# A two-layer perceiver block on one core: the small stages of each half of the batch cut into numbered fine slots, TensorE one pair behind, and half 1's first part moved among half 0's second part

## The chip, the core and the metric

The kernel runs on one core of a Trainium2 chip. Its time is in microseconds of the device (us); lower is better. Before the change three timed runs gave 323.14, 327.37 and 328.0 us, with a median of 327.37 us. Everything is float32.

## What is computed

The input is a batch of 16 sequences of 32 tokens with 128 features, a context of 512 keys for each sequence, and a mask over the keys. Six blocks follow each other, each with a layer norm ahead and a residual behind it:

```python
x = x + L0_xattn(layernorm(x), ctx)        # 16 heads of 8; query i sees its own 16 keys only
x = x + L0_attn(layernorm(x))              # time mixing, projections k, v, r, a scan over 32 steps
x = x + L0_ffn(layernorm(x))               # 8 experts of 64 (top 2 by sqrt(softplus)) and a shared one
x = x + L1_xattn(layernorm(x), ctx, mask)  # full attention, 16 heads, 512 keys
x = x + L1_attn(layernorm(x))              # linear attention with relu features, then a gelu layer of 512
x = x + L1_ffn(layernorm(x))               # 16 experts of 512, top 1, capacity 32 tokens
```

The scan keeps a running maximum o and two sums p and q, and gives `(A p + B v) / (A q + B)`, multiplied by a sigmoid of r.

## The kernel before

The program is written engine by engine, with semaphores by hand; each engine works strictly through its own list. The batch is cut into two halves of 8 sequences (256 tokens, two tiles of 128). Stretches of heavy work alternate on TensorE, and the small stages of a half (chains of little steps that go from engine to engine) are woven into them:

- `local(h)` is the first attention of half h: for each sequence a product on VectorE (L746), the softmax, a widened probability (L312), and the context product on TensorE (L1184). Between them stand the projections of the context to keys and values (`projection`, L1147 and L1151), 32 in all; the last 9 of them come after `local(1)`.
- `small_stages(h)` holds the rest of layer 0 and the queries of layer 1. Its first part is the residual and norm, the mixes (L809), the scans (L814, L830, L834) and the quotient with its reciprocal (L844). Its second part is the projection back, norm, the router (L860 to L890), the experts' hidden layer (Silu, L581), their second layer (L1302 to L1305), norm and the query (L1314, L912, L913).
- `full` is the attention of layer 1 over 64 units (4 heads of one sequence each), two to a pair, 32 pairs. For a pair: scores on TensorE (L1334), mask and minimum on VectorE (L941), the exponential on ScalarE (L601), four transposes per unit on TensorE (L1344), a copy by ScalarE (L608) or VectorE (L950), and three pairs later the product with the values (L1359). `take_heads` (L922, L924) empties the bank of outputs every eight pairs.
- `linear_stages(h)` is the rest of layer 1 from the inverse sums of the softmax (L966, L1383) through linear attention, the gelu layer (L1442, Gelu at L637, L1451, Gelu at L641) and the gate (L1040 to L1053) to the slots of the dispatch.
- A tail of 16 experts ends the program (L1535 to L1562).

The small stages are Python generators on each engine: each `yield` ends a coarse step, and the surrounding loop decides when the next one is written into the list. There is a step for each unit of `full` on every engine at the same place of the loop, so that TensorE, ScalarE, VectorE and GpSimd reach a step at about the same time and wait inside it for each other:

```python
if u < UNITS:
    advance(second, 1)
if u == UNITS - 1:
    finish(second)
if u >= LINEAR:
    advance(first, 1 if u % 5 != 4 else 0)
```

Here `second` is half 1's small stages, in units 0 to 31, and `first` half 0's linear stages, from unit 40. Half 0's small stages go into `local(1)`, and what is left of them stands behind it alone; half 1's stand whole in `full`; half 0's linear stages stand in the second part of `full` up to the gate, and what is left goes into `last_stages` with half 1's. `keep_warm` writes matmuls without use (L1498) where TensorE is otherwise alone with a chain. The banks X, Y and Z take the small products of both halves in turn.

## Time and profile before

| | us |
|---|---|
| median of three runs | 327.37 |
| the profiled execution's own time | 319.62 |
| its span, first to last instruction | 317.6 |
| TensorE busy | 281.4 (89%) |
| VectorE busy | 189.4 (60%) |
| ScalarE busy | 139.3 (44%) |
| GpSimd busy | 27.9 (9%) |
| mean granted clock of TensorE | 0.936 of full speed |

PE is TensorE, DVE VectorE, ACT ScalarE, POOL GpSimd. PEclk is the clock granted to TensorE as a share of 2.4 GHz; it has two levels, 2.4 and 1.2 GHz, so a stretch with a mean of c ran (1 - c) times 2 of its length at the lower one. A float32 matmul shows as several passes, so counts in the trace are twice those of the program. A bracket at a row's end is the idle time of the engine just before it, and what ended it.

### The profile page before, as it was taken

The page shows a single profiled execution, that of the slowest core. Times are in us where ns is not written, and L with a number is a line of the kernel's source. Part 1 is how long each engine was busy: PE and PEld are TensorE (multiplying, and loading weights), DVE is VectorE, ACT ScalarE, POOL GpSimd, SP SyncE. Part 2 cuts the span into 40 slices and gives each one's busy share as a digit, 9 for nine tenths or more (in the row PEclk, how much of TensorE's full clock was granted, in tenths as well). Part 3 has the DMA queues.
Part 4 walks back from the last instruction along what each step waited for, and adds up shares of the span by engine and source line. Part 5 has one row for each costly group of instructions (what it writes and reads, how often), then busy time and mean ns, then how long its engine had stood idle before and what let it go on. Part 6 is the DMA issues. An engine that isn't in the chain of part 4 may idle for free.

```text
span 317.6 us, 5216 instructions
## 1 busy us (share of the span) xinstructions
PE 281.4 (89%) x1990; PEld 181.5 (57%) x1990; DVE 189.4 (60%) x507; ACT 139.3 (44%) x296; POOL 27.9 (9%) x47
## 2 busy tenths in 40 slices
PE   8998999687988866997989999988899959979996
PEld 6325876166877543554566555454556528667766
DVE  3555265877443487975454668776753774742572
ACT  1215533454650374579713677375368800132130
POOL 4000000000030400013001200000100001010000
PEclk9999999999997999599565999999969989999999
DMA  7999290000019100050005000000000294000001
GB/s 288 427 439 398 66 198 3 0 1 2 0 43 417 70 1 2 0 134 0 0 3 132 3 0 2 2 1 0 2 0 2 91 436 169 1 2 0 0 2 35
DMA packets 3400, 26.79 MB, mean 84 GB/s; under 512 B 432, under 2 KB 1456, under 8 KB 1840
## 3 DMA queue, kind: packets, MB, share of 16 engines
q1 hardware_dynamic: 3376, 26.47, 23.0%
q8 instruction: 16, 0.26, 0.3%
q14 instruction: 8, 0.07, 0.1%
HBM read 26.20 MB, written 0.26 MB: 83 GB/s over the span
## 4 chain that ended last, share of the span: by engine, by line
PE 41%; DVE 9%; issue 5%; ACT 5%; POOL 1%; POOLq 0%; DVEq 0%; ACTq 0%
PE bank L1344 8%; PE bank L1334 8%; PE bank L1359 5%; PE bank L1498 3%; PE bank L1128 1%; PE bank L1305 1%; PE bank L1562 1%; PE bank L1417 1%; PE bank L1383 1%; PE bank L1553 1%; PE bank L1535 1%; PE bank L1442 1%; PE bank L1118 1%; ACT L601 1%; ACT work_sb L601 1%
## 5 line engine op out<-in xcount | busy, mean ns | idle before, releaser
L601 ACT ACTIVATE work_sb<-work_sb,small_sb 128x512 f32<-128x512 f32 x48 | 34.7, 722 | 45.6 <-DVE small_sb L941 45.4
L941 DVE CUSTOM_DVE_ANT_0 work_sb<-bank,mask_sb 128x512 f32<-128x512 f32 x48 | 31.9, 689 | 17.3 <-PE bank L1334 16.8
L1334 PE MATMUL bank<-k_sb,work_sb 32*128 32x512 f32 x128 | 40.2, 706 | 0.6 <-DVE small_sb L941 0.5
L1344 PEld LDWEIGHTS bank<-early_sb,work_sb 128*128 128x128 f32 x192 | 22.4, 151 | 30.3 <-issue 16.6
L1344 PE MATMUL bank<-early_sb,work_sb 128*128 128x128 f32 x192 | 33.9, 305 | 1.1 <-ACT work_sb L608 1.1
L374 POOL TENSOR_TENSOR rstd_sb<-veps_sb,minus_half_sb 128x2 f32<-128x2 f32 (+1 forms) x13 | 10.1, 774 | 214.9 <-DVE veps_sb L701 171.3
L1359 PE MATMUL bank<-work_sb,v_sb 128*32 128x128 f32 x512 | 22.6, 300 | 4.5 <-DVE otmp_sb L922 2.8
L608 ACT COPY work_sb<-bank 128x512 f32<-128x512 f32 x40 | 22.7, 568 | 6.6 <-PE bank L1344 6.6
L1498 PE MATMUL bank<-early_sb 128*128 128x256 f32 x98 | 25.0, 397 | 0.0
L950 DVE COPY work_sb<-bank 128x512 f32<-128x512 f32 x24 | 16.5, 688 | 11.5 <-PE bank L1344 9.8
L1498 PEld LDWEIGHTS bank<-early_sb 128*128 128x128 f32 x98 | 18.9, 203 | 3.1 <-issue 0.8
L746 DVE SCALAR_TENSOR_TENSOR work_sb<-bank,early_sb,work_sb 128x512 f32<-128x512 f32 x16 | 12.0, 749 | 14.4 <-PE bank L1207 13.9
L1359 PEld LDWEIGHTS bank<-work_sb,v_sb 128*32 128x32 f32 x512 | 13.4, 116 | 10.7 <-issue 7.9
L1151 PEld LDWEIGHTS bank<-late_sb,ctx_sb 128*128 128x128 f32 x128 | 16.2, 191 | 3.5 <-issue 3.4
L1147 PE MATMUL bank<-ctx_sb,early_sb 128*128 128x512 f32 x32 | 15.9, 615 | 1.7 <-ACT k_sb L503 1.7
L1151 PE MATMUL bank<-late_sb,ctx_sb 128*128 128x128 f32 x128 | 17.1, 277 | 0.3 <-DVE v_sb L784 0.2
L1207 PE MATMUL bank<-ctx_sb,early_sb 128*128 128x512 f32 x32 | 16.1, 604 | 0.2 <-DVE work_sb L746 0.2
L503 ACT ACTIVATE k_sb<-bank,early_sb 128x512 f32<-128x512 f32 x16 | 10.7, 684 | 9.8 <-PE bank L1147 9.7
L1334 PEld LDWEIGHTS bank<-k_sb,work_sb 32*128 32x128 f32 x128 | 10.6, 202 | 7.0 <-issue 4.6
L523 ACT COPY work_sb<-bank 128x512 f32<-128x512 f32 x16 | 9.4, 586 | 10.7 <-PE bank L1184 10.7
L1344 PE MATMUL bank<-early_sb,spare_sb 128*128 128x128 f32 x64 | 11.4, 307 | 2.6 <-ACT work_sb L608 2.6
L312 DVE TENSOR_TENSOR work_sb<-bank,early_sb 128x512 f32<-128x512 f32 x16 | 10.1, 684 | 5.9 <-PE bank L1171 3.2
(234 smaller groups left out, 454.3 us busy)
## 6 DMA issues: line engine op xcount, KB each, us to landing
ctx_sb<-moe_w SPq DMA_DIRECT2D x1, 4096.0 KB, 12.0
k_sb<-moe_w SPq DMA_DIRECT2D x1, 4096.0 KB, 13.6
ctx_sb<-ctx SPq DMA_DIRECT2D x3, 1024.0 KB, 14.1
late_sb<-late SPq DMA_DIRECT2D x1, 2895.0 KB, 20.6
mask_sb<-ctx_tok SPq DMA_DIRECT2D x1, 2048.0 KB, 12.3
v_sb<-ctx_tok SPq DMA_DIRECT2D x1, 2048.0 KB, 26.9
mask_sb<-mask SPq DMA_DIRECT2D x4, 512.0 KB, 8.1
mask_sb<-mask SPq DMA_DIRECT2D x8, 256.0 KB, 4.6
```

The costliest lines, as they stand in the source:

```text
L601: s.activation(sc[u % NSC], sc[u % NSC], ACT.Exp, bias=smin[:, u:u + 1], scale=-1.0, accum_out=rsum[:, u:u + 1]).then_inc(sig("p1_ready"), 1)
L608: s.copy(pt[j % NPT], bank[2 + j % NT][:, :]).then_inc(sig("pT_act"), 1)
L746: v.scalar_tensor_tensor(prod[c % HB].rearrange("p (q j) -> p q j", j=LOCAL), bank[c % 2][:, :].rearrange("p (q j) -> p q j", j=LOCAL), wt ...
L941: v.tensor_tensor_reduce(sc[u % NSC], bank[SB[u % NS]][:, :], mask[:, KEYS * b:KEYS * (b + 1)], MASK_BIG, 3e38, ALU.add, ALU.min, smin[:, ...
L950: v.tensor_copy(pt[j % NPT], bank[2 + j % NT][:, :]).then_inc(sig("pT_dve"), 1)
L1147: last = mm(dst[:, :], wt("wk1"), ctx[:, KEYS * b:KEYS * (b + 1)], start=True, stop=True)
L1151: last = mm(dst[:, P * k:P * (k + 1)], ctx[:, at:at + P], wt("wv1"), start=True, stop=True)
L1207: mm(bank[c % 2][:, :], wt("wk0"), ctx[:, KEYS * c:KEYS * (c + 1)], start=True, stop=True).then_inc(sig("k0_ps"), 1)
L1334: mm(bank[SB[u % NS]][:, :], qc[b][r, :], k1[r, KEYS * b:KEYS * (b + 1)], start=True, stop=True)\
L1344: last = nc.tensor.transpose(bank[2 + u % NT][:, P * k:P * (k + 1)], sc[u % NSC][:, P * k:P * (k + 1)], wt("ident"))
L1359: last = mm(bank[4][r, at:at + P], vkey[:, b, k, r], pt[(GROUPS * b + g) % NPT][:, P * k:P * (k + 1)], start=(k == 0), stop=(k == KT - 1), ...
L1498: mm(bank[2][:, 0:256], wt("ident"), wt("wv0")[:, 0:256], start=True, stop=True)
```

## The change

Every `yield` of the small and linear stages is replaced by `yield from rest(n)`, so that a stage has a number of fine slots, and the same piece of work has a number that agrees over the engines: 70 slots for the small stages, 63 for the linear ones. Long steps are cut (the norm into three pieces, the reciprocal into two, the scaled hidden tiles into two pairs, and so on). The loops now give three slots to a pair, and TensorE does the slots of pair v in round v + 1:

```diff
-        def beside(u, second, first):
-            if u < UNITS:
+        LOCAL_SLOTS = 3
+        SMALL_MIXED, SMALL_SLOTS = 27, 70
+        LOCAL_DONE = LOCAL_SLOTS * HB + 3 + 2 * (HB - NE + 1)
+        LINEAR_FROM, LINEAR_TO = 2 * HB + LATE_OUT, PAIRS + 1
+        def beside(v, i, second, first):
+            if v <= PAIRS // 2 - 2:
                 advance(second, 1)
-            if u == UNITS - 1:
-                finish(second)
-            if u >= LINEAR:
-                advance(first, 1 if u % 5 != 4 else 0)
+                if v == PAIRS // 2 - 2 and i == 2:
+                    finish(second)
+            if LINEAR_FROM <= v <= LINEAR_TO:
+                advance(first, 1)
+        def both_small(first, second, then):
+            for k in range(SMALL_SLOTS - LOCAL_DONE):
+                advance(first, 1)
+                if k < SMALL_MIXED:
+                    advance(second, 1)
+                then(k)
+            finish(first)
         def last_stages(first, second):
-            for k in range(STAGES):
+            for k in range(LINEAR_SLOTS):
                 advance(second, 1)
-                if k in (4, 8, 11):
+                if k % 5 in (0, 2, 4):
                     advance(first, 1)
+                if k == LINEAR_SLOTS // 2:
+                    finish(first)
             finish(second)
...
-            local(1, stages, pace_local)
-            finish(stages)
+            local(1, small0)
+            both_small(small0, small1, lambda k: projection() if k % 3 == 1 and nproj[0] < len(PROJ) else None)
             first = linear_stages(0)
-            full(small_stages(1), first)
+            full(small1, first)
```

`LOCAL_DONE` is 37: half 0's small stages have done 37 slots when `local(1)` ends. `both_small` then writes the 33 left, each followed (for the first 27) by a slot of half 1, and a context projection in every third. In `full` the remaining 43 slots of half 1 stand at pairs 0 to 14, and the first 45 slots of half 0's linear stages at pairs 19 to 33 (up to the gelu layer's second product); the other 18 slots go into `last_stages`, three in five of half 1's slots.

On TensorE the loop of `full` becomes:

```diff
+                    if 1 <= w <= LINEAR_TO + 1:
+                        beside(w - 1, 0, second, first)
                     if LATE_OUT <= w < PAIRS + LATE_OUT:
                         outputs((w - LATE_OUT) // 2, (w - LATE_OUT) % 2)
-                    if w <= PAIRS:
-                        beside(2 * w, second, first)
-                        if w:
-                            turn(2 * w - 1)
-                        beside(2 * w + 1, second, first)
+                    if 1 <= w <= LINEAR_TO + 1:
+                        beside(w - 1, 1, second, first)
+                    if 1 <= w <= PAIRS:
+                        turn(2 * w - 1)
+                    if 1 <= w <= LINEAR_TO + 1:
+                        beside(w - 1, 2, second, first)
```

To let two halves stand among each other, buffers are doubled: half 1's first part uses banks 0 and 1 in place of X and Y, the hidden tiles and the transposed weights have a place for each half, the linear stages use bank 3 and X or Y by half for their last products, and the residual semaphores are counted by half. On ScalarE the logarithm and all five Silu now stand in one slot:

```diff
                 act.wait_ge(sig("w_ready"), h + 1)
                 s.activation(fr[4], fr[3], ACT.Ln).then_inc(sig("ln_ready"), 1)
-                yield
-                for n in range(5):
-                    act.wait_ge(sig("hid_ps"), 3 * h + (1, 1, 2, 2, 3)[n])
+                silu(0, X[:, 0:HTOK], 2)
+                silu(1, X[:, HTOK:], 2)
+                silu(4, Y[0:H0, HTOK:], 1)
+                silu(2, X[:, 0:HTOK], 3)
+                silu(3, X[:, HTOK:], 3)
```

Three places show what this does to the lists. The first is VectorE between the experts of half 0 and the first scores. Before (L898 scales the hidden tiles, L734 to L715 are residual and norm, L912 and L913 the query, L941 the first unit of `full`):

```order
L893 COPY mask_sb<-bank 8x256
L898 TENSOR_TENSOR mask_sb<-mask_sb,bank 128x256 x4
L734 TENSOR_TENSOR x_tok_sb<-bank,xb_tok_sb 128x256
L694 BN_STATS stats_sb<-x_tok_sb 128x6 x2
L697 BN_AGGR aggr_sb<-stats_sb 128x2 x2
L701 TENSOR_SCALAR veps_sb<-aggr_sb 128x2
L715 TENSOR_SCALAR xn_tok_sb<-x_tok_sb,aggr_sb,rstd_sb 128x128 x2
L912 TENSOR_SCALAR work_sb<-bank,late_sb 128x256
L913 TENSOR_SCALAR work_sb<-work_sb 128x256
L941 ISA work_sb,small_sb<-bank,mask_sb 128x512
```

The same place after, from the second pair of scaled tiles on (mask_sb rows are half 1's scan stage, L745 is a projection's copy):

```order
L867 TENSOR_TENSOR otmp_sb<-otmp_sb,bank 128x256 x2
L790 TENSOR_TENSOR mask_sb<-mask_sb 128x8x32
L795 TENSOR_TENSOR mask_sb<-mask_sb 128x8x32
L796 SCALAR_TENSOR_TENSOR mask_sb<-mask_sb 128x264
L799 TENSOR_TENSOR mask_sb<-mask_sb 128x256
L800 SCALAR_TENSOR_TENSOR mask_sb<-mask_sb 128x264
L745 COPY v_sb<-bank 128x512
L693 TENSOR_TENSOR x_tok_sb<-bank,xb_tok_sb 128x256
L648 BN_STATS stats_sb<-x_tok_sb 128x6 x2
L802 TENSOR_TENSOR mask_sb<-mask_sb 128x256
L803 TENSOR_TENSOR mask_sb<-mask_sb 128x256
L654 BN_AGGR aggr_sb<-stats_sb 128x2 x2
```

Half 1's scans moved in between half 0's scaled tiles and its residual, and its sums in between the pieces of the norm.

The second is ScalarE at half 1's router. Before (L573 is the logarithm, L581 the five Silu, L601 an exponential of `full`):

```order
L571 ACTIVATE small_sb<-small_sb 128x16
L573 ACT_TABLE_LOAD
L573 ACTIVATE small_sb<-small_sb 128x16
L601 ACT_TABLE_LOAD
L601 ACTIVATE work_sb,small_sb<-work_sb,small_sb 128x512
L581 ACT_TABLE_LOAD
L581 ACTIVATE mask_sb<-bank,late_sb 128x256 x4
L581 ACTIVATE mask_sb<-bank,late_sb 64x256
L601 ACT_TABLE_LOAD
L601 ACTIVATE work_sb,small_sb<-work_sb,small_sb 128x512
```

And after (L551 the logarithm, L557 the Silu, L575 the exponential):

```order
L575 ACTIVATE spare_sb,small_sb<-spare_sb,small_sb 128x512
L551 ACT_TABLE_LOAD
L551 ACTIVATE small_sb<-small_sb 128x16
L557 ACT_TABLE_LOAD
L557 ACTIVATE mask_sb<-bank,late_sb 128x256 x2
L557 ACTIVATE mask_sb<-bank,late_sb 64x256
L557 ACTIVATE mask_sb<-bank,late_sb 128x256 x2
L575 ACT_TABLE_LOAD
L575 ACTIVATE work_sb,small_sb<-work_sb,small_sb 128x512
```

The exponential between the logarithm and the Silu is gone, and with it one load of a table; the others stand in one block.

The third is TensorE at the end of `full`. Before (L1359 outputs, L1467 the gate of half 0, L1383 the start of half 1's linear stages):

```order
L1359 MATMUL bank<-work_sb,v_sb 32x128 x8
L1467 MATMUL bank<-late_sb,lnT_sb 128x16 x2
L1344 MATMUL bank<-early_sb,work_sb 128x128 x8
L1359 MATMUL bank<-work_sb,v_sb 32x128 x8
L1344 MATMUL bank<-early_sb,spare_sb 128x128 x4
L1359 MATMUL bank<-work_sb,v_sb 32x128 x16
L1383 MATMUL bank<-mask_sb,late_sb 32x256 x4
```

And after (L1335 outputs, L1426 and L1438 the two products of the gelu layer of half 0, L1362 the start of half 1's linear stages):

```order
L1335 MATMUL bank<-work_sb,v_sb 32x128 x8
L1426 MATMUL bank<-lnT_sb,late_sb 128x256 x4
L1335 MATMUL bank<-work_sb,v_sb 32x128 x8
L1438 MATMUL bank<-late_sb,mask_sb 128x128 x8
L1362 MATMUL bank<-mask_sb,late_sb 32x256 x4
L1478 MATMUL bank<-early_sb 128x256 x2
```

The gelu layer of half 0 moved from the middle of the last pairs to behind the last scores, and half 0's gate is no longer in `full`.

## Rows read from the trace of the kernel before

**Rows 1.** The busy time of each engine by stage of the program.
```profile
core 0: us, PE busy (x) PEld busy (x) DVE busy (x) ACT busy (x) POOL busy (x), PEclk, DMA share, GB/s
...
81.65:108.23 26.58, 23.85 (x137) 19.61 (x136) 10.76 (x35) 10.00 (x17) 5.06 (x5) 0.94 0.39 158
108.23:183.66 75.43, 66.39 (x464) 39.00 (x463) 50.75 (x146) 43.41 (x101) 10.58 (x16) 0.82 0.12 29
183.66:195.05 11.39, 11.29 (x114) 6.07 (x113) 8.76 (x22) 8.34 (x22) 0.00 (x0) 1.00 0.00 0
195.05:256.85 61.80, 54.51 (x479) 32.78 (x478) 40.55 (x117) 36.91 (x84) 3.11 (x4) 0.94 0.09 35
256.85:299.63 42.78, 36.67 (x188) 28.39 (x187) 22.77 (x76) 7.48 (x15) 3.11 (x4) 0.96 0.19 81
```

**Rows 2.** Two stretches of the first pairs, same columns.
```profile
120.00:133.50 13.50, 10.94 (x84) 6.05 (x84) 12.53 (x29) 7.03 (x17) 0.72 (x1) 0.75 0.00 0
147.60:174.35 26.75, 23.46 (x128) 15.13 (x125) 12.29 (x37) 13.07 (x28) 2.80 (x3) 0.62 0.17 39
```

**Rows 3.** TensorE in order of time: start, us, engine, line, tiles, count.
```profile
149.67 0.65 PE L1281 MATMUL bank<-lnT_sb,late_sb 128*64 128x256 f32 x2 [2.05 <-ACT mask_sb L581]
151.08 2.08 PE L1334 MATMUL bank<-k_sb,work_sb 32*128 32x512 f32 x4
...
180.79 1.13 PE L1334 MATMUL bank<-k_sb,work_sb 32*128 32x512 f32 x4
...
230.67 0.65 PE L1359 MATMUL bank<-work_sb,v_sb 128*32 128x128 f32 x16 [1.93 <-DVE otmp_sb L922]
```

**Rows 4.** ScalarE at half 1's logarithm and Silu; four such loads stand there.
```profile
143.82 1.28 ACT L573 ACT_TABLE_LOAD   x1
...
148.78 2.04 ACT L581 ACTIVATE mask_sb<-bank,late_sb 128x256 f32<-128x256 f32 x5
```

**Rows 5.** VectorE during half 1's first part: all, then L941, then L950.
```profile
110.59:134.40 23.81, 20.60 (x56) 0.86 0.00 1
110.59:134.40 23.81, 6.63 (x22) 0.86 0.00 1
110.59:134.40 23.81, 2.15 (x4) 0.86 0.00 1
```

**Rows 6.** VectorE's longest waits in half 0's second part.
```profile
90.34 0.29 DVE L882 TENSOR_TENSOR mask_sb<-small_sb 128x128 f32<-128x128 f32 x1 [3.02 <-POOL small_sb L439]
...
101.75 0.42 DVE L734 TENSOR_TENSOR x_tok_sb<-bank,xb_tok_sb 128x256 f32<-128x256 f32 x1 [5.04 <-PE bank L1305]
```

**Rows 7.** TensorE on half 1's first part: L1128, then L1247, in one stretch.
```profile
109.20:120.00 10.80, 0.71 (x4) 1.00 0.01 2
109.20:120.00 10.80, 1.56 (x6) 1.00 0.01 2
```

**Rows 8.** VectorE at the end of `full`: all, then L941, then L950.
```profile
242.80:257.29 14.49, 9.79 (x35) 1.00 0.38 145
242.80:257.29 14.49, 3.92 (x12) 1.00 0.38 145
242.80:257.29 14.49, 2.07 (x3) 1.00 0.38 145
```

**Rows 9.** TensorE: half 0's gate, the last outputs, and a gelu layer's second product.
```profile
249.37 0.59 PE L1118 MATMUL bank<-early_sb,xn_tok_sb 128*128 128x128 f32 x2 [0.29 <-DVE xn_tok_sb L715]
...
252.11 0.62 PE L1467 MATMUL bank<-late_sb,lnT_sb 128*128 128x16 f32 x4
...
255.77 1.08 PE L1359 MATMUL bank<-work_sb,v_sb 128*32 128x128 f32 x32 [0.88 <-DVE work_sb L950]
259.94 2.07 PE L1383 MATMUL bank<-mask_sb,late_sb 128*32 128x256 f32 x8 [3.09 <-DVE mask_sb L966]
...
286.83 2.05 PE L1451 MATMUL bank<-late_sb,mask_sb 128*128 128x128 f32 x16
```

794 lines of the change are left out of this document (373 added, 421 removed).

## The prediction

> **What bounds the kernel now.** I read the busy time of each engine by stage first [rows 1]; the limits differ between the stages. To 81.65 us the two local attentions run, which the change touches only in where half 0's steps stand. From 81.65 to 108.23 TensorE works on half 0's second part and on projections. From 108.23 to 256.85 `full` runs: 16 pairs with half 1's small stages (75.43 us), 4 pairs with nothing beside them (11.39 us), and 12 pairs with half 0's linear stages and the last outputs (61.80 us). Half 1's linear stages end at 299.63, and the tail of 17.97 us to the end of the span is not touched.
>
> The four bare pairs tell what a pair costs: 11.39 / 4 = 2.85 us, with TensorE busy for 11.29 of 11.39. So `full` is bound by TensorE where nothing stands in its way. I therefore split its 148.62 us into work at full clock, idle time of TensorE, and time lost to the clock. Idle is 75.43 - 66.39 = 9.04, 0.10, and 61.80 - 54.51 = 7.29: 16.4 us. A stretch at half clock takes twice its time, so the loss is (1 - granted clock) times the stretch: 0.18 x 75.43 = 13.6, and 0.06 x 61.80 = 3.7: 17.3 us. What is left, 114.9 us, is work. The 33.7 us of idle and clock are what the change can win in `full`.
>
> Where they come from stands in the order of time. The clock was 0.75 from 120.0 to 133.5 and 0.62 from 147.6 to 174.35 [rows 2]; at 151.08 the four passes of a pair's scores took 2.08 us, at 180.79 1.13 us [rows 3]. The longer stretch began while TensorE waited 2.05 us at L1281 for ScalarE, which stood at its Silu between loads of tables [rows 3, 4]. At 230.67 TensorE had waited 1.93 us for `take_heads`, which stood on VectorE behind a whole norm that waited for GpSimd [rows 3]. These are coarse steps in which one engine waits for the next, and everything queued behind the wait waits too.
>
> **`full`.** What leaves: half 1's first part. On TensorE that is 0.71 (L1128) + 0.59 (one turned norm, priced by the row at 249.37) + 1.56 (three mixes) = 2.9 us [rows 7, 9]. Half 0's gate leaves too, 0.59 + 0.62 = 1.2 us [rows 9]. Work falls to 114.9 - 4.1 = 110.8 us. No matmul is added; three slots a pair instead of two units a pair only spread the same ones.
>
> Idle: TensorE's slots stand a pair later than those of the others, so their results have about one pair, 2.85 us, to arrive. Against that, VectorE now waits for TensorE's answer in the same way, but behind its wait stand only the second unit's minimum and one copy, while the next scores need just the first unit's minimum. Load is no limit: VectorE was busy 50.75 of 75.43 us and loses half 1's first part. One stall I can name stays: ScalarE has the logarithm, five Silu and the return to the exponential in one block. By the rows it takes 3 x 1.28 (loads) + 0.2 (the logarithm over 16 columns, an estimate: under the 0.4 us of one Silu) + 2.04 = 6.1 us [rows 4], and the last two Silu wait for a product that TensorE may only start after the first two. TensorE has about 2.9 us of other work meanwhile, so some 3 to 4 us are lost. For the rest I take half of what there was; idle 10 us in all. Its ends: 5 us (little but that block) and 16.4 us (nothing gained).
>
> Of tables, each load here took 1.28 us and the next instruction followed at once [rows 4]. The Trainium skill (ScalarE: Activation LUTs, What ACT_TABLE_LOAD costs) states about 2.66 us for each switch, a drain included. By it the block would be 3 x 2.66 + 2.3 = 10.2 us, as an estimate from that page, and the stall some 4 us longer; the trace disagrees with it. The same page (Table sets) has logarithm and exponential in one set, so that moving the logarithm would save nothing; here both directions cost a load.
>
> Clock: half of the causes go (the first part with its scans, the norm ahead of `take_heads`, and ScalarE's three further switches for the gelu layer, which now stands behind the last exponential). The ScalarE block may bring the clock down once more. I take 9 us of the 17.3; the ends are 3 and 17.3. So `full` takes 110.8 + 10 + 9 = 129.8 us, 18.8 less than now.
>
> **Half 0's second part, now with half 1's first.** VectorE was busy 10.76 of 26.58 us here [rows 1]. It gets half 1's first part: 20.60 - 6.63 - 2.15 = 11.8 us [rows 5]. The sum, 22.6 us, still fits in 26.6, and its waits are long enough to hold it: 5.04 us for the experts' products and 3.02 us for GpSimd's power are the largest [rows 6]. But the order is fixed, and half 1's steps also stand right ahead of steps on which half 0 depends, for instance the scans ahead of the residual and the sums between the pieces of the norm. If two thirds are covered, a third of 11.8 shows: +4 us. TensorE's 2.9 us go into its own waits, instead of matmuls without use. Ends: 0 (all covered) and 11.8 + 2.9, about +15 (nothing covered). I take 4, since the 15.8 us in which VectorE had nothing are more than what comes.
>
> **Half 1's linear stages.** They get the 18 last slots of half 0's. On VectorE that is 9.79 - 3.92 - 2.07 = 3.8 us [rows 8], beside 22.77 of 42.78 busy [rows 1]: half of it on the chain, 1.9 us. At the start the chain ran from the last outputs at 256.85 to L1383 at 259.94, an idle wait of 3.09 us [rows 9]. Now half 0's second gelu product (2.05 us by the row at 286.83) stands between, behind a load of 1.28 us and four gelu on ScalarE, so L1383 comes about 1.6 us later. Together +3.5 us; ends 0 and 8.
>
> **The local attention.** Half 0's steps are finer and some stand earlier; nothing is added. 0, between -2 and +2.
>
> **The sum.** -18.8 + 4 + 3.5 + 0 = -11.3 us. Against the profiled execution's own 319.62 us (2.0 more than its span) this gives 308.3. That execution was 7.8 us faster than the median of the three runs, 327.37; the difference taken off the median gives 316.1, and I predict 316.
>
> **Rivals.**
> - *The clock stays.* Low clock comes again at the ScalarE block and at the thin products of the router, since no matmul that follows it changed. For it: both times that half 0 or half 1 reached its experts, the stage showed less than full clock (0.94, 0.62 [rows 1, 2]). Against it: the pairs stand thicker around them. Loss stays 17.3: `full` gains 148.6 - (110.8 + 10 + 17.3) = 10.5, the sum is -10.5 + 7.5 = -3.0, so 324.4.
> - *Two chains in one line.* In the mixed stage each in-order engine stands at the one half's wait while the other half's work is ready behind it, so that the chains add up rather than overlap. Half 1's first part took 23.8 us in `full` [rows 5]; all of it on top of 26.6 costs +23.8. Sum: -18.8 + 23.8 + 3.5 = +8.5, so 335.9, slower. It decides from the point where the mixed stage is over 26.6 + 15.3 = 41.9 us long. For it: the fixed order. Against it: 15.8 us without work on VectorE, and slots whose numbers leave two to six slots between a request and its use.
> - *All of it.* Idle 5, clock 3, the mixed stage +2 and the last +1.5: `full` 118.8, sum -29.8 + 3.5 = -26.3, so 301. Against it: the ScalarE block alone makes idle time.
>
> **How the numbers follow.** My forecast has 0.55, with its own range 310 to 323; the clock stays 0.23; two chains in one line 0.10; all of it 0.12. The range from 305 to 329 takes in most of the second and the upper half of the last. A measurement here can tell about 2% from no change, so faster means under 320.8 and slower over 333.9. Faster is most of the forecast (0.48), all of it (0.12) and a little of the clock case (0.03): 0.63. Slower is the line of two chains, 0.10; the rest, 0.27, is within 2%.
>
> **What would show it.** In the profile after: the first scores at 112 us rather than 108; `full` near 130 us, with TensorE idle about 10 us of it and a granted clock around 0.93; the idle row ahead of the second hidden product (L1247 of the new program) 2 us or more; from the end of `full` to the end of the linear stages 46 us. Wrong would be: a mixed stage over 42 us long, a clock under 0.90 in the first 16 pairs, or idle time of TensorE on VectorE's minima (L915) of more than 5 us, which would say that VectorE now waits too long between a pair's two units.

## The result and the profile after

The changed kernel took 332.32 us, the median of four runs (332.00 to 333.74); the kernel before, run beside it, took 326.05 (323.14 to 328.00). The ratio is 1.031, with a 95% interval from 1.025 to 1.037: slower, where faster by three to four per cent was predicted, and outside the range of 305 to 329. Single executions of one kernel can be several per cent longer at a lower granted clock, so each ratio, here and below, sets only the executions without that against such ones of the kernel before, while the medians are over all; where a run had a single one of them, no ratio is given.

The sum of the prediction was made against one profiled execution, and so is this one. I cut both traces at four events on TensorE: the end of the last product with the values of `local(1)`, the first scores, the end of the last outputs, and the last dispatch. The busy time of the changed kernel between them, and in two stretches of its first pairs:

```profile
core 0: us, PE busy (x) PEld busy (x) DVE busy (x) ACT busy (x) POOL busy (x), PEclk, DMA share, GB/s
84.06:135.80 51.74, 37.71 (x165) 29.90 (x163) 22.24 (x64) 12.82 (x25) 7.59 (x7) 0.80 0.16 62
135.80:264.39 128.59, 117.31 (x1019) 67.79 (x1018) 84.16 (x236) 80.22 (x191) 10.36 (x11) 0.93 0.16 50
264.39:312.32 47.93, 43.45 (x224) 34.64 (x224) 26.41 (x95) 10.08 (x20) 3.81 (x5) 0.96 0.12 51
159.89:170.00 10.11, 9.25 (x40) 5.11 (x40) 3.37 (x11) 6.89 (x15) 1.41 (x1) 0.54 0.00 0
177.00:183.50 6.50, 6.50 (x34) 3.04 (x32) 4.39 (x9) 2.59 (x6) 0.00 (x0) 0.55 0.00 0
```

And of the kernel before, from the same event (in the prediction the stage was cut 0.9 us later, [rows 1]):

```profile
80.75:108.23 27.48, 24.75 (x139) 20.03 (x139) 10.76 (x35) 10.48 (x18) 5.06 (x5) 0.94 0.38 153
```

| part | before | after | difference | predicted |
|---|---|---|---|---|
| to the end of the values | 80.75 | 84.06 | +3.3 | 0 (-2 to +2) |
| half 0's second part, in the new program with half 1's first | 27.48 | 51.74 | **+24.3** | +4 (0 to +15) |
| `full` | 148.62 | 128.59 | **-20.0** | -18.8 |
| half 1's linear stages | 42.78 | 47.93 | +5.1 | +3.5 (0 to +8) |
| tail and what lies around the span | 20.0 | 20.0 | 0 | 0 |
| profiled execution | 319.62 | 332.32 | +12.7 | -11.3 |

So `full` came out as forecast, almost to the microsecond, and the stage ahead of it gave all of that back and more. Of the 24.0 us between forecast and result, 20.3 are one term.

That term splits as `full` was split in the prediction. Before: idle 27.48 - 24.75 = 2.7 us, lost to the clock 0.06 x 27.48 = 1.6, work 23.1. After: idle 51.74 - 37.71 = 14.0, clock 0.20 x 51.74 = 10.3, work 27.4. Idle time of TensorE makes 11.3 of the 24.3, the clock 8.7, work 4.3. Keep-warm products count as work here: they were busy for 11.7 us of this stage, against 4.8 before, and so hide some of the waiting.

TensorE in that stage, in order of time: start, us, engine, line, tiles, count, and in brackets the idle time before and what ended it. L1247 is the experts' hidden layer, L1141 a projection of values, L1478 the keep-warm products, L1262 the turned coefficients, L1268 their spread, L1276 to L1279 the experts' second layer, L1103 a turned norm, L1310 the first scores.

```profile
85.98 1.11 PE L1247 MATMUL bank<-lnT_sb,late_sb 128*128 128x256 f32 x4
...
94.25 2.08 PE L1247 MATMUL bank<-lnT_sb,late_sb 128*128 128x256 f32 x4 [3.67 <-ACT spare_sb L557]
...
104.30 0.58 PE L1262 MATMUL bank<-early_sb,small_sb 128*8 128x128 f32 x2 [0.76 <-DVE small_sb L858]
...
114.92 0.79 PE L1276 MATMUL bank<-late_sb,work_sb 8*128 8x128 f32 x2 [2.92 <-DVE otmp_sb L867]
...
121.67 3.45 PE L1478 MATMUL bank<-early_sb 128*128 128x256 f32 x8
124.96 1.95 PE L1141 MATMUL bank<-late_sb,ctx_sb 128*128 128x128 f32 x16
130.83 0.58 PE L1103 MATMUL bank<-early_sb,xn_tok_sb 128*128 128x128 f32 x2 [3.92 <-DVE xn_tok_sb L672]
...
135.80 1.13 PE L1310 MATMUL bank<-k_sb,work_sb 32*128 32x512 f32 x4
```

VectorE in the same stage. L745 is a projection's copy, L768 half 1's first mix (it waits for the turned norm that ScalarE copies, L483), L850 the router's comparison, L867 the second pair of scaled tiles, L693 the residual behind the experts:

```profile
93.14 0.17 DVE L843 SCALAR_TENSOR_TENSOR small_sb<-small_sb 128x16 f32<-128x16 f32 x1
100.32 0.42 DVE L768 TENSOR_TENSOR mask_sb<-mask_sb 128x256 f32<-128x256 f32 x1 [7.00 <-ACT mask_sb L483]
...
101.19 0.68 DVE L745 COPY v_sb<-bank 128x512 f32<-128x512 f32 x1
101.78 0.28 DVE L850 TENSOR_TENSOR small_sb<-small_sb 128x128 f32<-128x128 f32 x1
...
114.12 0.74 DVE L867 TENSOR_TENSOR otmp_sb<-otmp_sb,bank 128x256 f32<-128x256 f32 x2
...
126.12 0.69 DVE L745 COPY v_sb<-bank 128x512 f32<-128x512 f32 x1 [7.97 <-PE bank L1141]
126.73 0.41 DVE L693 TENSOR_TENSOR x_tok_sb<-bank,xb_tok_sb 128x256 f32<-128x256 f32 x1
```

Read the last two rows with TensorE's. The experts' products ended at 121.67, and the residual needs nothing else. But ahead of it in VectorE's list stands a projection's copy; its product stands on TensorE behind the experts and eight passes of keep-warm products, and the copy could start at 126.12. So the residual started 5.1 us after it could have, and the 3.92 us wait of TensorE at 130.83 is that loss seen from the other side. At 101.78 the router's comparison stands behind a copy and behind half 1's mix, 8.5 us after the last step before it, of which GpSimd's power needs about 3 (it ended VectorE's wait of 3.02 us there before [rows 6]). Which of the two holds it up these rows do not say; e1 does.

ScalarE (L498 is a projection's copy, L548 the router's exponential, L551 the logarithm, L557 a Silu):

```profile
89.72 0.69 ACT L498 ACTIVATE k_sb<-bank,early_sb 128x512 f32<-128x512 f32 x1 [4.84 <-PE bank L1137]
90.31 0.20 ACT L548 ACTIVATE small_sb<-small_sb 128x16 f32<-128x16 f32 x1
90.53 1.28 ACT L551 ACT_TABLE_LOAD   x1
91.83 0.22 ACT L551 ACTIVATE small_sb<-small_sb 128x16 f32<-128x16 f32 x1
92.06 1.28 ACT L557 ACT_TABLE_LOAD   x1
93.36 0.84 ACT L557 ACTIVATE spare_sb<-bank,late_sb 128x256 f32<-128x256 f32 x2
```

The exponential's input was ready at 86.6 (VectorE's last step for it), but a projection's copy that waited 4.84 us stood ahead of it; its product stood on TensorE behind half 1's first product and its keep-warm products. Then the second hidden product waited 3.67 us for the Silu, since both pairs now share one bank. In the kernel before they had a bank each, and in half 0 no wait stood at the second.

### The profile page after: what moved, and what is told of

It is laid out like the page before. It is cut to its first block, busy times and chain, and to the rows that moved or that the text cites. A ratio compares the mean times of both kernels' runs of the same rounds, so it can differ in the third digit from the quotient of the medians.

```text
span 330.3 us, 5275 instructions
## 1 busy us (share of the span) xinstructions
PE 287.3 (87%) x2020; PEld 188.6 (57%) x2020; DVE 189.4 (57%) x511; ACT 135.6 (41%) x293; POOL 28.0 (8%) x47
## 4 chain that ended last, share of the span: by engine, by line
PE 46%; DVE 9%; issue 5%; ACT 3%; POOL 1%; POOLq 0%; DVEq 0%; ACTq 0%
PE bank L1320 9%; PE bank L1310 8%; PE bank L1478 6%; PE bank L1335 5%; PE bank L1279 2%; DVE work_sb L924 1%; PE bank L1410 1%; PE bank L1118 1%; PE bank L1542 1%; PE bank L1533 1%; PE bank L1515 1%; PE bank L1247 1%; PE bank L1391 1%; PE bank L1103 1%; ACT work_sb L575 1%
## 5 line engine op out<-in xcount | busy, mean ns | idle before, releaser
L575 ACT ACTIVATE work_sb<-work_sb,small_sb 128x512 f32<-128x512 f32 x48 | 34.7, 722 | 37.9 <-DVE small_sb L915 37.7
L1320 PEld LDWEIGHTS bank<-early_sb,work_sb 128*128 128x128 f32 x192 | 21.6, 147 | 33.1 <-issue 16.0
L1310 PE MATMUL bank<-k_sb,work_sb 32*128 32x512 f32 x128 | 38.4, 677 | 0.9 <-DVE small_sb L915 0.8
L1320 PE MATMUL bank<-early_sb,work_sb 128*128 128x128 f32 x192 | 32.8, 296 | 4.5 <-DVE work_sb L924 3.3
L1478 PE MATMUL bank<-early_sb 128*128 128x256 f32 x128 | 36.2, 427 | 0.0
L1478 PEld LDWEIGHTS bank<-early_sb 128*128 128x128 f32 x128 | 26.8, 221 | 4.2 <-issue 0.4
L1335 PE MATMUL bank<-work_sb,v_sb 128*32 128x128 f32 x512 | 21.5, 287 | 2.1 <-ACT work_sb L582 0.9
L500 ACT COPY v_sb<-bank 128x512 f32<-128x512 f32 x12 | 7.0, 584 | 30.6 <-PE bank L1141 30.6
L704 DVE SCALAR_TENSOR_TENSOR work_sb<-bank,early_sb,work_sb 128x512 f32<-128x512 f32 x16 | 12.0, 750 | 11.8 <-PE bank L1196 11.3
L1141 PEld LDWEIGHTS bank<-late_sb,ctx_sb 128*128 128x128 f32 x128 | 16.8, 200 | 2.6 <-issue 2.2
L1335 PEld LDWEIGHTS bank<-work_sb,v_sb 128*32 128x32 f32 x512 | 12.7, 112 | 9.1 <-issue 5.3
L1141 PE MATMUL bank<-late_sb,ctx_sb 128*128 128x128 f32 x128 | 17.2, 283 | 0.0
L498 ACT ACTIVATE k_sb<-bank,early_sb 128x512 f32<-128x512 f32 x16 | 10.7, 684 | 15.0 <-PE bank L1137 15.0
L1310 PEld LDWEIGHTS bank<-k_sb,work_sb 32*128 32x128 f32 x128 | 10.3, 197 | 7.7 <-issue 5.2
L575 ACT ACTIVATE spare_sb<-spare_sb,small_sb 128x512 f32<-128x512 f32 x16 | 11.5, 719 | 7.3 <-DVE small_sb L915 7.3
```

Source lines behind the costliest of these rows:

```text
L575: s.activation(sc[u % NSC], sc[u % NSC], ACT.Exp, bias=smin[:, u:u + 1], scale=-1.0, accum_out=rsum[:, u:u + 1]).then_inc(sig("p1_ready"), 1)
L704: v.scalar_tensor_tensor(prod[c % HB].rearrange("p (q j) -> p q j", j=LOCAL), bank[c % 2][:, :].rearrange("p (q j) -> p q j", j=LOCAL), wt ...
L1141: last = mm(dst[:, P * k:P * (k + 1)], ctx[:, at:at + P], wt("wv1"), start=True, stop=True)
L1310: mm(bank[SB[u % NS]][:, :], qc[b][r, :], k1[r, KEYS * b:KEYS * (b + 1)], start=True, stop=True)\
L1320: last = nc.tensor.transpose(bank[2 + u % NT][:, P * k:P * (k + 1)], sc[u % NSC][:, P * k:P * (k + 1)], wt("ident"))
L1335: last = mm(bank[4][r, at:at + P], vkey[:, b, k, r], pt[(GROUPS * b + g) % NPT][:, P * k:P * (k + 1)], start=(k == 0), stop=(k == KT - 1), ...
```

## The experiments

Theory 1, from the trace: mixing the halves is what makes the stage long. Its rival: half 0's own chain is held up, by other work in the in-order lists (projections, keep-warm products) and by the Silu. Stages of each run's profile, cut as above (us):

| run | to the values' end | stage | `full` | linear | span | median | ratio to before |
|---|---|---|---|---|---|---|---|
| before | 80.75 | 27.48 | 148.62 | 42.78 | 317.6 | | |
| after | 84.06 | 51.74 | 128.59 | 47.93 | 330.3 | 332.32 | 1.031 |
| e1 unmixed | 86.62 | 42.83 | 155.64 | 48.51 | 351.5 | 341.86 | 1.057 [1.040, 1.075] |
| e2 projections earlier | 84.75 | 47.82 | 139.14 | 48.31 | 338.0 | 336.56 | 1.028 [1.007, 1.048] |
| e3 no keep-warm | 84.42 | 44.67 | 135.96 | 49.57 | 331.4 | 334.11 | 1.036 [1.027, 1.045] |
| e4 tail late | 84.73 | 51.62 | 128.60 | 46.41 | 329.3 | 330.56 | 1.025 [1.014, 1.035] |
| e5 projections placed | 84.85 | 44.47 | 129.25 | 48.31 | 324.8 | 326.13 | 1.007 [1.003, 1.012] |
| e6 a bank for the hidden product | 84.76 | 48.33 | 138.59 | 47.93 | 337.6 | 339.24 | none |
| e7 = e5 + e6 + e4 | 82.76 | 41.81 | 128.48 | 48.09 | 319.1 | 323.91 | 1.010 [1.001, 1.020] |
| e8 = e7, half 1 later | 84.86 | 40.42 | 140.38 | 49.02 | 331.7 | 331.66 | none |
| e9 quiet tail | 84.13 | 51.64 | 128.59 | 44.46 | 326.8 | 328.34 | 1.015 [1.010, 1.020] |
| e10 = e7, quiet chain | 82.93 | 41.29 | 129.20 | 48.00 | 319.4 | 320.85 | 0.990 [0.983, 0.997] |
| e11 = e10 + e9 | 84.17 | 41.28 | 132.33 | 46.37 | 322.1 | 325.49 | none |
| e12 = e1, placed | 83.09 | 34.46 | 146.40 | 48.31 | 330.2 | 339.07 | 1.052 [1.045, 1.059] |
| e13 all that helped | 84.02 | **38.15** | 128.43 | 44.84 | 313.4 | **315.65** | **0.986 [0.981, 0.991]** |
| e14 = e12, placed better | 84.91 | **27.90** | 154.10 | 48.93 | 333.8 | 330.95 | none |

The kernel before, timed again beside them, had medians from 321.49 to 324.99 us (324.99 beside e1 to e4, 324.83 beside e5 to e8, 323.36 beside e9 to e12, 321.49 beside e13 and e14), so a per cent between runs of different groups decides little. Median and ratio can part: in e7 the median is below that of the kernel before beside it, and the ratio is above 1.

Each stage comes from one profiled execution, and its clock need not be the edit's doing. For the comparison of stages I therefore also give the time at full clock, the stage's length times its granted clock: 25.8 us before, 41.4 after, 34.3 in e1, 35.1 in e7, 29.3 in e12, 33.2 in e13, 27.9 in e14.

### Is it the mixing? (e1)

Half 1's first part goes back into `full`, five slots to a pair there; its banks are X and Y again.

```diff
-        SMALL_MIXED, SMALL_SLOTS = 27, 70
+        SMALL_MIXED, SMALL_SLOTS = 0, 70
...
-                advance(second, 1)
+                advance(second, (2, 1, 2)[i])
```

> The changed kernel with the mixing alone undone: half 0's second part stands alone again in fine slots (banks X and Y again for half 1's first part), and all 70 slots of half 1 stand in full, five to a pair in place of three. Theory 1 (in the mixed stage the two chains add up, 51.8 us against 27.5 before): the stage falls back to 27 to 30 us, full gets longer by 2.9 us of TensorE's work and some 5 to 8 us of denser slots, so the median falls by 14 to 17 us to about 316 to 318. Theory 2 (the fine slots or TensorE's lag themselves cost the time): the stage stays over 40 us and the median over 328.

Theory 1 fell as the whole cause. Half 0's chain alone, with nothing of half 1 beside it, still took 42.83 us: mixing is worth 51.74 - 42.83 = 8.9 us (7.1 at full clock), and 15.4 us were left against the kernel before. Both numbers of theory 2 came, a stage over 40 us and a median over 328; what is in it, e5 to e14 have to say. The stage of e1, by engine:

```profile
86.62:129.45 42.83, 31.90 (x146) 25.65 (x145) 10.59 (x35) 10.35 (x18) 5.06 (x5) 0.80 0.13 49
```

VectorE and ScalarE do the same work here as before (10.59 and 10.35 us against 10.76 and 10.48), and still TensorE is idle for 10.9 us. VectorE's list has the same two places as the changed kernel, now without half 1:

```profile
102.03 0.69 DVE L745 COPY v_sb<-bank 128x512 f32<-128x512 f32 x1 [8.40 <-PE bank L1141]
102.63 0.28 DVE L850 TENSOR_TENSOR small_sb<-small_sb 128x128 f32<-128x128 f32 x1
...
122.37 0.69 DVE L745 COPY v_sb<-bank 128x512 f32<-128x512 f32 x1 [9.81 <-PE bank L1141]
122.97 0.41 DVE L693 TENSOR_TENSOR x_tok_sb<-bank,xb_tok_sb 128x256 f32<-128x256 f32 x1
```

The router's comparison starts 9.0 us after the last step before it (8.5 with half 1's mix there), and the residual 5.0 us after the experts' end at 118.0. So at both places it is the projection's copy that holds the chain up. The wait of 3.67 us at the second hidden product is there too.

### Projections, keep-warm products, and the tail (e2, e3, e4)

e2 puts a projection in every second slot instead of every third:

```diff
-            both_small(small0, small1, lambda k: projection() if k % 3 == 1 and nproj[0] < len(PROJ) else None)
+            both_small(small0, small1, lambda k: projection() if k % 2 == 1 and nproj[0] < len(PROJ) else None)
```

> The changed kernel with the nine context projections of the mixed stage in every second slot (slots 1 to 17) in place of every third (1 to 25), so that no projection and no copy stands between half 0's experts and its residual. Theory 1a (VectorE's residual at 126.7 us stood behind a copy at 126.1 that waited 8.0 us for a projection queued on TensorE behind useless matmuls): the residual comes 4 to 5 us sooner and the median falls by 4 to 6 us, to about 327. Rival (the chain of half 0 itself is that long, the copy only happened to stand there): within 1.5 us of 332.

The stage became 3.9 us shorter, so where projections stand matters. The time does not follow: the four executions were 329.71, 333.14, 339.97 and 340.05 us. In the last of them, which was profiled, `full` was 10.6 us longer, at a mean clock of 0.85 instead of 0.93; the shortest is 10 us shorter with the same edit, so this is not shown to be the edit's doing.

e3 has no keep-warm products in the stage:

```diff
-            alone[0] = True
+            alone[0] = False
             both_small(small0, small1, lambda k: projection() if k % 3 == 1 and nproj[0] < len(PROJ) else None)
```

> The changed kernel without the 32 useless matmuls (11.7 us of TensorE's time in the trace, 3.5 us of it right behind half 0's experts and 3.0 us right ahead of the first scores) in the mixed stage. Theory 1b (they stand in TensorE's line in front of work that others wait for, and the clock is low with them anyway, 0.80 in the stage): the stage is 4 to 7 us shorter, median about 327. Rival (they hold the clock up where it is up): the granted clock of the stage falls below 0.75 and the median is the same or up to 5 us longer.

The stage became 7.1 us shorter, a little more than theory 1b had, and `full` 7.4 us longer, so that the time is the rival's (334.11 us, all four executions within 1.4 us). The first two stretches of `full` in e3 show where:

```profile
129.09:145.00 15.91, 15.15 (x58) 7.73 (x58) 8.28 (x26) 6.92 (x17) 2.59 (x3) 0.50 0.52 165
145.00:160.00 15.00, 12.04 (x102) 7.04 (x99) 6.95 (x24) 9.80 (x22) 2.73 (x1) 0.96 0.01 1
```

TensorE ran the first 16 us of `full` at half clock; in the changed kernel the first 14.2 us ran at 1.00. Keep-warm products in this stage earn what they cost, at least some of them; e10 takes out a part.

e4 starts half 0's last linear slots in the tail at slot 14:

```diff
-                if k % 5 in (0, 2, 4):
+                if k >= 14 and k % 5 != 4:
                     advance(first, 1)
-                if k == LINEAR_SLOTS // 2:
+                if k == 38:
```

> The changed kernel with half 0's last 18 linear slots later among half 1's (four in five of slots 14 to 38 in place of three in five of slots 0 to 31). Theory 3 (the last stage is 5.1 us longer than before since half 0's gelu, residual, norm and gate stand in the in-order lines at half 1's own residual and norm at its start): the stage falls from 47.9 to 45 or 46 us, median 330 to 331. Rival (the time is lost wherever the slots stand, or at the start behind the second gelu product alone): within 1 us of 332.

The linear stages took 46.41 us, 1.5 less, and the median was 330.56, as theory 3 had it. But at full clock they are the longer ones (1.00 x 46.41 against 0.96 x 47.93 = 46.0), and the same edit in e7 gained nothing (48.09), so I put no weight on it.

### The lists put in order (e5 to e8)

e5 only moves the nine projections. `then(-1)` is called once ahead of the loop, and each engine has its own slots:

```diff
+            then(-1)
             for k in range(SMALL_SLOTS - LOCAL_DONE):
...
-            both_small(small0, small1, lambda k: projection() if k % 3 == 1 and nproj[0] < len(PROJ) else None)
+            both_small(small0, small1, lambda k: [projection() for at in (-1, -1, 6, 6, 7, 8, 12, 13, 15) if at == k])
```

The line shown is TensorE's; ScalarE has (2, 2, 6, 6, 7, 7, 12, 12, 15), VectorE (2, 2, 8, 8, 11, 11, 14, 14, 14).

> The changed kernel with the nine projections of the mixed stage put elsewhere among its slots and nothing else moved: two products ahead of TensorE's first slot, the other seven from slot 6 to 15 (behind hidden(2), the turned coefficients and the spread), none behind the experts; ScalarE's copies once ahead of the exponential and then behind the Silus, VectorE's none ahead of the router's comparison or of the residual behind the experts. Theory A (half 0's chain is held up by projections that stand in the wrong places of the in-order lines): the stage of 51.75 us becomes 42 to 45 (the residual follows the experts by 0.2 us and not 5, the first Silu starts 1.8 us sooner), and the time is 322 to 326. Theory B (it is held up by half 1's steps and by what the clock gives): the stage stays at 49 to 52 us and the time at 329 to 333.

Theory A held: the stage is 7.3 us shorter, `full` within 0.7 us, the time 326.13, 0.1 over the range. The residual follows the experts' end (121.46 on TensorE) by 0.3 us:

```profile
121.76 0.42 DVE L694 TENSOR_TENSOR x_tok_sb<-bank,xb_tok_sb 128x256 f32<-128x256 f32 x1 [3.06 <-issue]
```

e6 gives half 0's second hidden product a bank of its own:

```diff
-                        last = mm(X[:, HTOK * n:HTOK * (n + 1)], wt("rw1")[:, P * (at + n):P * (at + n + 1)], lnT[:, c],
+                        last = mm((X if h or not at else Z)[:, HTOK * n:HTOK * (n + 1)], wt("rw1")[:, P * (at + n):P * (at + n + 1)], lnT[:, c],
...
-                pe.wait_ge(sig("hid_ready"), 5 * h + 2)
+                if h:
+                    pe.wait_ge(sig("hid_ready"), 5 * h + 2)
```

> The changed kernel, but half 0's second hidden product goes to a bank of its own (bank 7; the keep-warm products of this stage go to bank 2), so that it waits for no Silu. Theory A: TensorE's wait of 3.67 us at that product goes, the stage is 3 to 6 us shorter (45.5 to 49 us) and the time 326 to 329. Theory B: the wait goes, but reappears at the turned coefficients, since ScalarE and VectorE reach them no sooner; the stage is within 1.5 us of 51.75 and the time within 330 to 333.

The stage is 3.4 us shorter, as theory A had it, but the time is longer: the four executions were 329.28, 338.86, 339.62 and 340.59 us. `full` shows why, here and at its worst stretch:

```profile
133.09:271.68 138.59, 128.04 (x1019) 73.74 (x1018) 84.13 (x236) 80.25 (x191) 10.08 (x10) 0.85 0.15 46
170.00:200.00 30.00, 28.67 (x164) 16.96 (x164) 12.53 (x35) 9.21 (x23) 1.39 (x2) 0.60 0.10 23
```

The same 1019 matmuls, idle time 10.6 us against 11.3, but 10.7 us more busy time: only the clock differs. The shortest execution, 329.28 us, had the same edit. For the stage the run counts, for the time it says little.

> Both edits together, with half 0's last linear slots in the tail begun at slot 14 (as e4). If the stage's loss is coupling in the lines, the gains add: stage 39 to 43 us, time 317 to 322, no slower than the kernel before. If the clock takes them back: 325 or more, with the lower clock in full.

e7 joins e4, e5 and e6. The stage is 41.81 us, 9.9 less than in the changed kernel; apart they gave 7.3 and 3.4. The median, 323.91 us, is 2 us over what was expected; by the ratio it is 1.0% above the kernel before, with an interval that almost reaches 1.

e8 starts half 1 five slots later (`if 5 <= k < SMALL_MIXED + 5`):

> As e7, but half 1's first part begins five slots later among half 0's second part, so that VectorE's wait for half 1's turned tiles stands behind half 0's comparison of the router. If half 1's step held up half 0's chain (the 7.0 us wait on VectorE at 100.32), the stage is 3 to 5 us shorter than in e7; if not, within 1 us of e7, or longer by what half 1 then ends later.

Stage 40.42 us, 1.4 less than e7, between the two numbers, with a new wait of 2.47 us for GpSimd's queries ahead of the first scores in it. All of the 1.4 is clock, though (0.92 against 0.84; at full clock 37.2 us against 35.1), so starting half 1 later gained nothing here. The profiled `full` had a clock of 0.85 again; three of four executions took 331.5 to 333.7 us, the fourth 322.69.

### Keep-warm products on the way, and the rest of half 0's chain (e9 to e12)

e9, in the linear stages of TensorE:

```diff
-                keep_warm(7)
+                keep_warm(7 if h else 0)
```

and the same for all the others there.

> The changed kernel without the keep-warm products that half 0's last linear slots bring into the tail; half 1's own keep-warm products stay. In the tail of the changed kernel 14 of half 0's passes (3.27 us at 279.54) and its scan with a wait of 1.13 us stood ahead of half 1's products. If these make the tail longer than before (from half 1's first linear product to the last dispatch 45.2 us against 39.7), it is 41 to 43 us now and the time 2 to 4 us less than 332.3. If something else does (the shared engines, the one-hot step), it stays at 44 to 46 us and the time at 331 to 333.

From half 1's first linear product to the last dispatch it is 41.7 us, against 45.2 in the changed kernel and 39.7 before; 1.5% slower than before instead of 3.1%. This is the piece of the changed kernel's tail that goes (L1451 is the gate's product and L1387 the first product of half 1 behind it; L1457 counts half 0's one-hot rows, L1410 is half 1's again):

```profile
279.18 0.51 PE L1451 MATMUL bank<-late_sb,lnT_sb 128*128 128x16 f32 x4
279.54 3.27 PE L1478 MATMUL bank<-early_sb 128*128 128x256 f32 x14
282.64 0.50 PE L1387 MATMUL bank<-late_sb,mask_sb 128*128 128x4 f32 x4
...
286.53 0.41 PE L1457 MATMUL bank<-small_sb,late_sb 128*128 128x32 f32 x2 [1.13 <-DVE small_sb L1042]
...
287.26 2.38 PE L1410 MATMUL bank<-mask_sb 128*128 128x32 f32 x16
```

The 14 passes stood behind half 0's gate to keep the clock while nothing was to be done; now half 1 stands behind them. The clock of the linear stages is 0.96 with them and without.

e10 is e7 without the keep-warm products at half 1's first slot, behind both hidden products and behind the turned coefficients.

> As e7 (projections placed, a bank for the second hidden product, late tail) without the keep-warm products at half 1's first slot, behind both hidden products and behind the turned coefficients; those behind the experts and around the query product stay. If they hold the chain up, the stage of 41.8 us in e7 becomes 38.5 to 40.5; if they only fill waits, it stays at 41 to 42. The clock theory adds: what the stage gains comes back as a lower clock in full, as in the run without any of them, so that the time stays within 1.5 us of e7's.

Stage 41.29 us, only 0.5 less than e7: most of these filled waits. `full` took 0.7 us more than in e7 (129.20 against 128.48), not 7 as in e3; its first 14.2 us had a clock of 0.88, against 1.00 in e7 and 0.50 in e3. That points at the products left, behind the experts and around the query product, as the ones that keep most of its clock; no run takes out only those. The ratio is 0.990 where e7 had 1.010, but the shortest executions (318.94 and 320.97 us) and the profiled ones (321.41 and 321.14) hardly differ, so this is no clear gain over e7.

> e10 and e9 together. If the two are independent and neither is given back: 316 to 320 us, faster than the kernel before by 1.5 to 3 per cent. If the clock gives back what the mixed stage gains: 320 to 323.

e11 (e9 and e10 together) spread from 318.92 to 334.22 us and decides nothing on the time; its linear stages took 46.37 us, 1.6 less than in e10, where the quiet tail alone gave 3.5. What stands between the two is e4's later start of half 0's slots, and e13, which goes back to the changed kernel's order, has 44.84.

> The unmixed version (half 1's first part is run in full, five slots a pair, as in e1) with the projections placed and the second hidden product in a bank of its own as in e7. Its stage has half 0's chain alone. If the misplaced projections and the wait for the Silu were all that made e1's stage 42.8 us against 27.5 us before, it is 29 to 32 us, and what e7's 41.8 us has beyond that is the price of mixing. If the fine slots cost by themselves, it is 35 us or more. The time is of less interest (full carries more): 325 to 340.

e12 lies between the two numbers. Half 0's chain alone, with projections placed and the bank, took 34.46 us: 8.4 less than in e1, and still 7.0 more than before (3.5 at full clock). Its VectorE list shows two copies that my own placing had left in bad slots:

```profile
93.33 0.29 DVE L852 TENSOR_TENSOR small_sb<-small_sb 128x128 f32<-128x128 f32 x1
95.30 0.69 DVE L746 COPY v_sb<-bank 128x512 f32<-128x512 f32 x1 [1.68 <-PE bank L1142]
95.91 0.28 DVE L856 TENSOR_TENSOR small_sb<-small_sb,late_sb 128x128 f32<-128x128 f32 x1
...
99.73 0.69 DVE L746 COPY v_sb<-bank 128x512 f32<-128x512 f32 x1 [2.69 <-PE bank L1142]
100.34 0.40 DVE L862 COPY work_sb<-bank 8x256 f32<-8x256 f32 x1
```

### The last 7 us, and the parts together (e13, e14)

e14 is e12 with five of VectorE's copies further on, (2, 2, 8, 8, 12, 12, 20, 20, 20) in place of (2, 2, 8, 8, 11, 11, 14, 14, 14), ScalarE's last at 20 in place of 15, and one of TensorE's products at 15 in place of 13, behind the spread.

> e12 with the better placement alone. In e12 a copy of 0.69 us that waited 1.68 us for its product stood ahead of the coefficients on VectorE (95.30), and another that waited 2.69 us ahead of their turned copy (99.73). If these make the last 7 us between e12's stage of 34.46 us and the 27.48 us before, it is 30 to 31.5 us, the rest being the experts at half clock. If the fine slots cost by something else, it is 33 us or more.

The stage is 27.90 us, under the lowest of what was expected, and the kernel before had 27.48:

```profile
84.91:112.81 27.90, 24.29 (x146) 19.82 (x145) 10.87 (x35) 10.13 (x18) 5.06 (x5) 1.00 0.35 142
```

Against e12 TensorE is idle for 3.6 us instead of 5.3, and the clock is 1.00 instead of 0.85: the experts' products took 3.9 us (102.39 to 106.29) where e12 had 7.0. So of the 6.6 us that moving these copies and the product made, 1.7 are idle time and about 5 are the clock, which came with it in this profile; that the moves brought it is not shown. At full clock the stage is 27.9 us against 25.8 before (idle 3.6 against 2.7, work 24.3 against 23.1), so the fine slots and the one slot for the logarithm and all the Silu cost at most 2.1 us together. The time of this version is no better (322.71 to 335.82 us), since `full` then holds half 1's first part.

> The changed kernel with what helped so far and one better placement: half 0's second hidden product in a bank of its own, no keep-warm products on half 0's chain nor from half 0's last slots in the tail (the tail's order as in the changed kernel), and the projections placed as in e5 but for the last ones: their products behind the spread and VectorE's copies behind the coefficients and behind the scaled tiles. Adding the parts (values end 83 to 84, stage 37 to 39, full 129, linear stages 44.5, rest 18): span 311.5 to 314.5, time 313.5 to 319, faster than the kernel before by 1.5 to 3 per cent. If the clock takes the gain back: 320 or more.

e13, in `full` as in the changed kernel, has 38.15 us in the stage, and its parts add up as expected: the median of 315.65 us (314.73 to 316.37, six runs) is 1.4% faster than the kernel before by the ratio, a little under the 1.5 to 3 expected, and all six runs lie below all twelve of the kernel before beside them (318.69 to 327.59). Against the changed kernel it is 4 to 5% less: 4.4% by the two ratios, 5.0% by the medians, which were not taken side by side. Its mixed stage and its linear stages by engine:

```profile
84.02:122.17 38.15, 30.25 (x150) 23.64 (x149) 22.11 (x64) 12.59 (x25) 7.30 (x7) 0.87 0.27 111
...
250.60:295.44 44.84, 41.31 (x210) 32.95 (x209) 26.28 (x95) 10.10 (x20) 3.82 (x5) 0.92 0.13 54
```

Mixing costs 38.15 - 27.90 = 10.3 us by e13 and e14 (e13 also lacks some keep-warm products), 41.81 - 34.46 = 7.4 by e7 and e12, and 8.9 by the changed kernel and e1; at full clock 5.3, 5.8 and 7.1. In return `full` is shorter: 128.48 us in e7 against 146.40 in e12, which has the same fine slots but keeps half 1's first part in `full`. That is 17.9 of the 20.0 us that `full` won over the kernel before.

## Why the prediction was wrong

**What bounds `full`, and its term: right in size.** It takes 128.59 us (129.8 forecast). By the same split: idle 11.3 (10 forecast), clock 0.07 x 128.59 = 9.0 (9), work 108.3 (110.8). The stall I named is there, 2.96 us at the second hidden product, and low clock follows it:

```profile
159.89 2.08 PE L1247 MATMUL bank<-lnT_sb,late_sb 128*128 128x256 f32 x4 [2.96 <-ACT mask_sb L557]
```

The page's cost groups show 0.8 us of idle time of TensorE on VectorE's minima in all, where over 5 would have told against the forecast. The last two windows of the first profile above have the clock at 0.54 and 0.55, the one behind this stall, the other 7 us later, behind half 1's spread (L1268 at 174.18).

Two things under this number are less right. One of the prediction's own signs of being wrong came: the first 16 pairs (135.80 to 202.47) had a clock of 0.87, under 0.90; the mean of 0.93 comes from the rest, at 1.00. (The forecast loss of 9 us, if it falls there, itself gives 0.87, so the sign was set too high.) And the source of the gain is the part that left. e12 keeps half 1's first part in `full`, at five slots to a pair: idle 146.40 - 129.04 = 17.4 us and clock 0.13 x 146.40 = 19.0, no better than the 16.4 and 17.3 before. That fine slots and the lag of a pair by themselves shorten the waits, no run shows.

**Half 0's second part with half 1's first: wrong, +24.3 for +4.** The step that failed is "If two thirds are covered, a third of 11.8 shows: +4 us". It prices only what half 1 brings on VectorE, against the time in which VectorE had nothing. Three things were missing or wrong in it.

- It took half 0's chain itself as given. But the change moved the nine projections to every third slot, and the second hidden product behind the Silu. I had named that wait for half 1 in `full` and not asked for it in half 0, where nothing else keeps TensorE busy. e1 against e14 prices the two together: 42.83 - 27.90 = 14.9 us, of which 8.6 are clock; at full clock 6.4, about as much as mixing. In the mixed stage itself, e5 gave 7.3 us and e6 3.4. One of these places, a projection's copy straight ahead of the residual, stood in the rows of the lists that I had printed.
- It took idle time for cover. A third of half 1's work was to show, 3.9 us; mixing costs 7.4 to 10.3 us, within the 0 to 15 that I gave, though about twice what I took or more. VectorE's busy time in the stage rose by 11.5 us, just as forecast (11.8), and it was still without work for 29.5 of 51.74 us. It was idle at a fixed place of its list.
- It had no term for the clock. The stage was at 0.94 before and at 0.80 after, 8.7 us. In e14 the chain is tight and the clock 1.00; in e1 idle time is 7.3 us more and the clock costs 8.6. That the waits bring the clock down is argued from such pairs; in e10 the clock is 0.79 with TensorE idle for 8.0 us, in e8 0.92 with 8.8.

**Half 1's linear stages: right in sign, +5.1 for +3.5.** The missing piece has a name: half 0's keep-warm products in the tail. e9 without them has 44.46 us, +1.7. The delay of half 1's first linear product was to be 1.6 us; it came 2.76 us after the last outputs (3.09 before), so that was no cost at all.

**The local attention: +3.3 for 0, outside its two ends.** It is there in every run of the new program (82.8 to 86.6 us to the end of the values). In the three profiles with a clock of 1.00 up to there (e7, e10, e12), as the kernel before has it, it is 2.0 to 2.3 us; the changed kernel has 0.98, which costs another 1 to 2 us. TensorE waits 2.78 us for ScalarE's copy of a projection at 64.28, where the kernel before waited 0.90:

```profile
64.28 3.89 PE L1137 MATMUL bank<-ctx_sb,early_sb 128*128 128x512 f32 x8 [2.78 <-ACT k_sb L498]
```

No run tried the slots in `local(1)`, so that this is their doing is argued, not shown.

**The rivals.** "Two chains in one line" had the outcome: a stage over 41.9 us, slower, 335.9 us. It had 0.10. Its mechanism is real but made only 8.9 of the 24.3 us, not 23.8; half 0's own chain and the clock had no rival of their own. "The clock stays" was wrong in size and right in place: in `full` the loss fell from 17.3 to 9.0 us, and the two low stretches that are left stand behind the ScalarE block and the router's thin products, as it had said. The stall block on ScalarE was read rightly: a load took 1.28 us, and the next instruction followed 0.02 us later (92.06 and 93.36). The Trainium skill (ScalarE: Activation LUTs, What ACT_TABLE_LOAD costs) has 2.66 us for a switch, about 1.28 of it the load and the rest a drain. The trace after has the load at 1.28 us and nothing of a drain (the first load began 0.02 us after the exponential's end at 90.51), as the trace before had.

**The chances.** Faster had 0.63 and slower 0.10. The range ended at 329 although the forecast's own bound for the mixed stage, +15 instead of +4, led to 327 by itself, before a lower clock or a tail of +8.

## What to carry to other kernels

When a change regroups the work of in-order engines, go through the new list of each engine around each step of the longest chain and ask of whatever stands directly ahead: when is its input ready? A copy of 0.69 us that waits for another engine held up the next step by 5 us here (5.1 in the changed kernel, 5.0 in e1), and moving nine projections made the stage 7.3 us shorter (e5). Measure one stage at one clock before you say what an edit won: of the 14.9 us between e1 and e14, 8.6 are the clock. Free time on an engine covers extra work only if the list is at that work when the time is free. And a product that is there only to keep the clock should go when its place is no longer a waiting place (e9: 3.5 us), while taking out all that stand ahead of a dense stretch cost 7.4 us in it (e3).

## What had not been expected of the hardware

The same `full`, 1019 matmuls in the same order with 10.5 to 12 us of idle time, took 128.4 to 129.3 us in seven profiles (after, e4, e5, e7, e9, e10, e13), 132.3 in one (e11) and 138.6 to 140.4 us in three (e2, e6, e8), with a granted clock of 0.92 to 0.93 in the seven, 0.90 in e11 and 0.85 in the three. Executions of a single kernel differ as much: e8 had 322.69 and 331.47 us, e6 329.28 and 338.86, e2 329.71 and 340.05. So the ten microseconds are not shown to come from the edits, and a single execution of such a kernel can mislead by 3% or more. What decides it is open; no run here isolates it.

The clock of half 0's stage went with TensorE's waits only roughly. In the changed kernel TensorE had keep-warm products for 11.7 us and no wait over 3.92 us, and the clock was 0.80; in e12, with no wait over 1.91 us, it was 0.85; in e14, with none over 1.36 us, 1.00. In e3, without keep-warm products, it was 0.76, and then 0.50 for the first 15.91 us of `full`, though TensorE was busy for 15.15 of them.
